# A four-layer recurrent and expert kernel: scan end by blocks, expert blocks early, gating of channel parts on GpSimd, shares applied after the hidden product

## The reference

```
# layer 0 mixer: sign-weight MLP, group quantisation, then a selective scan, 256 channels, 16 states
h = h * exp(dt * A) + (dt * x) * B          # per channel and state, along 1024 tokens
y = (sum over states of h * C + D * xs) * silu(z);   s = qx + y @ out_proj
# layer 0 ffn: 8 experts of three relu layers; v[e] = sum over tokens of y_e * w_e; g = ind @ v
# layer 1 mixer: two softmax-weighted sums over the tokens, then xn @ (Wq + diag(..) Wv.. Wr)
# layer 1 ffn: 8 experts, hidden 256, the best two of each token:
h = silu(xn @ Wgate_e) * (xn @ Wup_e);  g = sum over chosen e of share_e * (h @ W2_e)
```

## Time and profile before

| what | value |
|---|---|
| runs (median; all) | 1368.02 us; 1360.9, 1368.02, 1369.02 |
| the profiled execution | 1367.33 us, span 1365.3 us |
| TensorE busy | 1192.4 us (87%) |
| VectorE busy | 997.3 us (73%) |
| ScalarE busy | 801.6 us (59%) |
| GpSimd busy | 480.8 us (35%) |

### The profile page before, as it was taken

One profiled execution on the slowest core, in us unless ns is written; L12 is line 12 of the kernel. 1 busy time (PEld: TensorE's weight loads), 2 busy tenths in 40 slices (PEclk: granted clock), 3 DMA queues, 4 the chain that ended last, 5 costly groups with the idle time before them and its releaser, 6 DMA issues.

```text
span 1365.3 us, 14601 instructions
## 1 busy us (share of the span) xinstructions
PE 1192.4 (87%) x5025; PEld 626.3 (46%) x5025; DVE 997.3 (73%) x1432; ACT 801.6 (59%) x1097; POOL 480.8 (35%) x263
## 2 busy tenths in 40 slices
PE   5767599999985899999947999999999999798888
PEld 1322144444432444444525666666666666422454
DVE  4558799999986455533568899999899999623353
ACT  4344666676642434322466888888888888634542
POOL 9000188888876000000001354544544445500000
PEclk9879599999995899999778999999999999999999
DMA  3000255555531000000000000000000000000000
GB/s 115 0 3 6 89 182 183 180 192 188 183 137 47 0 0 1 1 0 0 0 0 16 14 14 21 15 21 14 14 21 14 21 14 14 1 0 0 1 0 31
DMA packets 26073, 59.90 MB, mean 44 GB/s; under 512 B 5544, under 2 KB 11080, under 8 KB 25736
## 3 DMA queue, kind: packets, MB, share of 16 engines
q1 hardware_dynamic: 26000, 58.97, 12.9%
HBM read 56.80 MB, written 1.38 MB: 43 GB/s over the span
## 4 chain that ended last, share of the span: by engine, by line
PE 41%; DVE 37%; ACT 15%; issue 5%; POOL 1%; DMA 0%; DVEq 0%; POOLq 0%; SPq 0%; ACTq 0%
DVE work L585 10%; DVE work L1371 6%; DVE work L1390 5%; ACT ps L487 5%; PE ps L869 5%; PE ps L877 4%; PE ps L1025 4%; PE ps L885 4%; ACT work L1232 3%; DVE yd L1435 3%; ACT work L1227 3%; PE ps L1066 2%; DVE work L1438 2%; PE ps L1626 1%; PE ps L235 1%
## 5 line engine op out<-in xcount | busy, mean ns | idle before, releaser
L1491 POOL TENSOR_TENSOR ssum<-ssum,rs 128x1024 f32<-128x1024 f32 x32 | 77.1, 2410 | 221.3 <-DVE work L1371 219.0
L585 DVE TENSOR_TENSOR_SCAN work<-ps,work 128x1024 f32<-128x1024 f32 x64 | 146.6, 2291 | 8.8
L605 POOL TENSOR_TENSOR work<-work 128x1024 f32<-128x1024 f32 x43 | 102.5, 2384 | 116.9 <-DVE work L585 116.9
L1371 DVE SCALAR_TENSOR_TENSOR work<-work,w_t 128x1024 f32<-128x1024 f32 x96 | 123.4, 1285 | 24.2 <-ACT work L1232 21.9
L409 PE MATMUL ps<-work,ident 128*128 128x512 f32 x256 | 123.0, 603 | 2.5 <-POOL work L605 2.4
L487 ACT ACTIVATE ps<-work,A 128x1024 f32<-128x1024 f32 x64 | 71.6, 1119 | 83.3 <-DVE work L585 81.7
L901 ACT ACTIVATE work<-ps 128x512 f32<-128x512 f32 x64 | 38.2, 597 | 110.8 <-PE ps L869 110.8
L1499 POOL TENSOR_TENSOR yd<-yd,work 128x896 f32<-128x896 f32 x32 | 67.3, 2102 | 72.9 <-DVE work L1438 72.9
L937 DVE TENSOR_TENSOR work<-work,ps 128x512 f32<-128x512 f32 x64 | 44.0, 688 | 57.0 <-PE ps L877 57.0
L1485 POOL MEMSET ssum<- 128x2048 f32 x1 | 1.8, 1804 | 237.2 <-DVE work L257 237.2
L1414 DVE SCALAR_TENSOR_TENSOR work<-work,ps 128x64 f32<-128x64 f32 x384 | 79.3, 276 | 6.2
(11 more groups left out here) (340 smaller groups left out, 2669.0 us busy)
## 6 DMA issues: line engine op xcount, KB each, us to landing
work<-bc_rows SPq DMA_DIRECT2D x43, 512.0 KB, 3.6
yd<-bc_rows SPq DMA_DIRECT2D x21, 512.0 KB, 3.5
rs<-w_rows SPq DMA_DIRECT2D x32, 256.0 KB, 3.4
w_t<-in_tile_w SPq DMA_DIRECT2D x32, 195.5 KB, 2.4
work<-in_w SPq DMA_DIRECT2D x1, 2048.0 KB, 9.6
shared<-in_f SPq DMA_DIRECT2D x3, 512.0 KB, 6.1
work<-in_x SPq DMA_DIRECT2D x4, 256.0 KB, 3.5
work<-in_w2e SPq DMA_DIRECT2D x1, 1024.0 KB, 11.6
```

Of the source, the lines that this page charges most:

```text
L585: dve.tensor_tensor_scan(h, flat_pair(DABANK), h, 0.0, ALU.mult, ALU.add).then_inc(m0["scan"], 1)
L605: pool.tensor_tensor(HS[u % 4], HS[u % 4], CB[u % 3], ALU.mult).then_inc(m0["state"], 1)
L1371: c = dve.scalar_tensor_tensor(HC[u], HP[:, tap:tap + SEQ], par(u, "taps", tap), HC[u], ALU.mult, ALU.add)
L1491: pool.tensor_tensor(ssum[:, b, :], ssum[:, b, :], rs[:, :, :].rearrange("p k t -> p (k t)"), ALU.add).then_inc(m2["ss"], 1)
```

## The change

1. Three expert blocks of layer 0 (`AHEAD` = 6 half steps) are computed before the loop, between the projection and the x_proj matmuls; ScalarE's relus of them stand around its silus of `XS`. In the loop all expert work runs six half steps ahead. The buffer r3 is doubled, and GpSimd weighs a block three units before ScalarE sums it.
2. Within the loop ScalarE scales `XS[:, j]` by D (at state 3), and GpSimd adds `DX` and multiplies by silu(z) for j = 0, 1, 2 while the next part is scanned (at its states 4 and 6). Part 3 is done by VectorE after the loop in two halves.
3. The end of the scan, out_proj, mix, gating and the second norm run block by block: blocks 0 and 1 first, blocks 2 and 3 inside the norm's steps (`first=`).
4. Layer 1: the bfloat16 share broadcast, `xw` and the split into parts are gone. The shares are turned with one transpose, stored to DRAM and loaded again, spread over the partitions, one 512-token row for each step; GpSimd multiplies the hidden product by them (128x1024) before the output matmuls, which now run five steps later (`LAG` = 5, eight hidden buffers). The gate and up matmuls of step 0 are issued inside the norm.
5. `stairs` is cut into 12 parts that GpSimd issues before its multiplication at even steps of the expert loop.
6. The expert weights of layer 1 are loaded as soon as the last decay is done; the last two gatings overlap the loop.

```diff
@@ l0_pe
+            for v in range(AHEAD):
+                f0_experts_pe(pe, v)
             for k in range(NB):
                 b, h = divmod(k, NB // BATCH)
                 pe.wait_ge(m0["act"], m0["xs"] + MI * (b + 1))
...
-                f0_experts_pe(pe, u)
+                f0_experts_pe(pe, u + AHEAD)
                 if u >= 1:
                     add_up(u - 1)
+            f0_turn_pe(pe)
+            for k in range(2):
+                f0_mix_pe(pe, k)
+            pe.wait_ge(m0["drive"], len(UNITS))
+            for k in range(2):
+                out_project(pe, k)
+            for k in range(2, NB):
+                f0_mix_pe(pe, k)
             add_up(len(UNITS) - 1)
@@ l0_act
+                if j == 0:
+                    for v in range(AHEAD // 2):
+                        f0_relus_act(act, v)
+                if j == 1:
+                    for v in range(AHEAD // 2, AHEAD + 1):
+                        f0_relus_act(act, v)
                 act.wait_ge(m0["dve"], m0["conv"] + j + 1)
                 act.activation(XS[:, j, :], DL[:, j, :], ACT.Silu).then_inc(m0["act"], 1)
...
+                if n == 3:
+                    j = MI * b + m
+                    act.activation(XS[:, j, :], XS[:, j, :], ACT.Copy, scale=V("d", m)).then_inc(m0["xs_scaled"], 1)
@@ l0_pool
+                if j >= 0 and n == 4:
+                    pool.wait_ge(m0["xs_scaled"], j + 1)
+                    pool.wait_ge(m0["act"], m0["sum_out"] + j + 1)
+                    pool.tensor_tensor(XS[:, j, :], XS[:, j, :], DX[:, j, :], ALU.add).then_inc(m0["y_sum"], 1)
+                if j >= 0 and n == 6:
+                    pool.wait_ge(m0["y_sum"], j + 1)
+                    pool.tensor_tensor(XS[:, j, :], XS[:, j, :], zgate[j % MI][:, (j // MI) * SEQ:(j // MI + 1) * SEQ],
+                                       ALU.mult).then_inc(m0["y_gated"], 1)
                 pool.wait_ge(m0["scan"], u + 1)
@@ new: l0_last_dve, l0_rest_dve (run inside the norm of layer 1)
+        def l0_last_dve(dve, own):
+            j = BATCH * MI - 1
+            dve.wait_ge(m0["ysum"], len(UNITS))
+            dve.wait_ge(m0["xs_scaled"], j + 1)
+            for h in range(NB // BATCH):
+                here = slice(h * BL, (h + 1) * BL)
+                own(dve.tensor_tensor(XS[:, j, here], XS[:, j, here], ps[:, YACC + h, :], ALU.add))
+                dve.tensor_tensor(XS[:, j, here], XS[:, j, here], zgate[MI - 1][:, ...],
+                                  ALU.mult).then_inc(m0["y_half"], 1)
+        def l0_rest_dve(dve, own, k):
+            if k == 1:
+                l0_last_dve(dve, own)
+            if k >= 2:
+                l0_out_dve(dve, own, k)
@@ new: l1_pool
+            for n in range(N1):
+                if n % 2 == 0 and n // 2 < STAIRS:
+                    stairs(pool, own, n // 2)
+                pool.wait_ge(f1["h"], 2 * (n + 1))
+                pool.wait_ge(share_in[n % len(share_bc)], 16 * (n // len(share_bc) + 1))
+                pool.tensor_tensor(hid[n % NH], hid[n % NH], share_bc[...].unsqueeze(1).to_broadcast([P, 2, BL]),
+                                   ALU.mult).then_inc(f1["weighed"], 1)
@@ l1_pe
+            norm_pe(pe, 3, X, f0["dve"], f0["x_out"], logits, rest)
+            pe.wait_ge(m1["dve"], m1["sub"] + 1)
+            l1_side_pe(pe, 0)
+            for n in range(1, N1 + LAG):
+                if n < N1:
+                    gates(n)
+                    ups(n)
+                if n == 1:
+                    pe.wait_ge(f1["dve"], f1["shared"] + 1)
+                    pe.transpose(ps[:, TURN_BANK, 0:P], by_expert, ident[:, :]).then_inc(f1["pe"], 1)
+                if n >= LAG:
+                    outputs(n - LAG)
                 l1_side_pe(pe, n)
@@ l1_dve
+            top2(dve, own, rw[:, 0], rt[:, :, 0:E])
+            hidden(0)
+            chosen_share(dve, own, rw[:, 0], 1e-6)
+            dve.tensor_tensor(by_expert..., rw[:, 1], bc(rm[:, 2, :]), ALU.mult).then_inc(f1["dve"], 1)
+            for n in range(1, N1):
+                hidden(n)
                 l1_side_dve(dve, own, n)
```

More of the change, by code:

```diff
@@ L212, in build @@
                     dve="sub:1 wk_scaled:2 wv_scaled:2 comb_out:2", each="soft_mm less_max exp weighted")
-        f1 = stages("f1", pe="picked_T:1", act="g:4", dve="picked:1 x_out:4", each="rt_out wbc xw gate silu up h y")
+        f1 = stages("f1", pe="shares_T:1", act="g:4", dve="shared:1 x_out:4", each="rt_out rows w_in0 w_in1 w_in2 w_in3 gate silu up h weighed y")
         m2 = stages("m2", pe="dt_mm:1 bc_mm:8 cum:1 tot:1 cumT:1 bt:4 gt:4 rms:4",
@@ L252, in norm_pe, with norm_dve @@
                     use(k)
-        def norm_dve(dve, own, r, src, dst, gain=None, bias=None):
+        def norm_dve(dve, own, r, src, dst, gain=None, bias=None, first=None):
             def scale(k):
@@ new lines, in l1_pe, with gates, ups, outputs @@
+        def l1_pe(pe):
+            def gates(n):
+                k, e = divmod(n, E)
+                for m in range(2):
+                    if n >= 1:
+                        pe.wait_ge(f1["silu"], 2 * (n - 1) + m + 1)
+                    c = e * 2 * I1 + m * P
+                    pe.matmul(ps[:, GATE_BANK[m], :], W["w13"][:, c:c + P], blk(XN, k), start=True, stop=True).then_inc(f1["gate"], 1)
+            def ups(n):
+                k, e = divmod(n, E)
+                for m in range(2):
+                    if n >= 1:
+                        pe.wait_ge(f1["h"], 2 * (n - 1) + m + 1)
+                    c = e * 2 * I1 + I1 + m * P
+                    pe.matmul(ps[:, UP_BANK[m], :], W["w13"][:, c:c + P], blk(XN, k), start=True, stop=True).then_inc(f1["up"], 1)
+            def outputs(q):
+                k, e = divmod(q, E)
+                if e == 0 and k >= 2:
+                    pe.wait_ge(f1["act"], f1["g"] + k - 1)
+                pe.wait_ge(f1["weighed"], q + 1)
+                for m in range(2):
+                    mm = pe.matmul(ps[:, Y_BANK[k % 2], :], W["w2e"][:, (2 * e + m) * P:(2 * e + m + 1) * P], hid[q % NH][:, m, :],
+                                   start=(e == 0 and m == 0), stop=(e == E - 1 and m == 1))
+                mm.then_inc(f1["y"], 1)
@@ L850, in logits @@
                     mm = pe.matmul(ps[:, SIDE, i * E:(i + 1) * E], tile(XN, i), W["router"], start=True, stop=True)
+                if k == 1:
+                    pe.wait_ge(load["experts"], 16 * len(EXPERTS))
+                    gates(0)
+                if k == 2:
+                    ups(0)
                 if k == NB - 1:
                     mm.then_inc(m1["pe"], 1)
[L854 to L856 removed]
```

378 lines of the change are left out of this document (194 added, 184 removed).

## The result

The changed kernel takes **1356.64 us** (median of 7 runs, 1352.57 to 1358.82) against 1367.74 us for the kernel before in the same session (7 runs, 1360.9 to 1370.24). The ratio is 0.9928, 95% interval 0.9905 to 0.9951: faster by 0.7%, clear of noise, but inside the 1% that the prediction counted as "the same" (it had given that 0.37, and 0.55 to faster by more). Forecast were 1353.0 us, a range of 1335 to 1370, and 15 us of gain; 11.1 us came. The profiled execution has a span of 1354.6 us (before: 1365.3).

The account below looks back on a forecast made before the run. It saw VectorE pacing the scan loop, no engine full from scan end to router, and matmuls bounding the expert loop; 2.2 + 3.2 - 14.5 - 5.5 - 0.3 = -15 us gave 1353 us, range 1335 to 1370.

Parts of the forecast that it names:

- A: Ahead of the scan: three expert blocks placed there delay x_proj and so VectorE; +2.2 us, between 0 and +6.
- B: Scan loop: pace stays, but lateness from GpSimd's added multiplications partly reaches VectorE; +3.2 us in sum.
- C: Scan end to router: block-by-block work takes 33.5 us in place of 48.0; -14.5 us, between -17 and -9.
- D: Router to the end of the expert loop: earlier start and shorter steps, less new waits; -5.5 us in all.
- E: Last gatings: three of four run before the last outputs; -0.3 us, between 0 and -2.
- the lock: Expert loop: VectorE's weighing of two SBUF operands waits for GpSimd's hidden multiplication; 8.2 us, between 0 and 19.
- The clock's +1.1: Expert loop: two falls of TensorE's clock cost +3.5 us, a warmer start gives -2.4; +1.1 us.
- (4): Expert loop: side work loses its one-step lead, so TensorE waits at eight steps for the weighing; 17.8 us.
- Rivals 1: Whole kernel: short steps overlap and nothing is held up; 19 us better, 1334; chance 0.30 together with halfway, 1344.
- 4 (1335): Expert loop: the eight waits don't exist since the weighing finishes earlier; 17.8 us better, 1335; chance 0.05.
- Rival 3: Expert loop: the clock falls after each of eight waits, 41 us in place of 3.5; 1391, slower; chance 0.08.
- Rival 2: Expert loop gives back nearly everything: GpSimd's lock costs 19 us, scan-to-router gains only 11; 1367, no change; chance 0.20.

Follow-up runs that it names:

- e8: Changed kernel with the removed constant selr (a memset and three selections on GpSimd) put back at the start, used by nobody: 1358.64 us.
- e6: Changed kernel with the addition and gating of parts 0 to 2 moved from GpSimd's loop to VectorE behind the last scan: 1356.38 us.
- e16: Changed kernel with 3 and 4 extra matmuls, results unused, in TensorE's two waits of the second norm: 1345.97 us.
- e2: Changed kernel with expert 0's gate and up matmuls of layer 1 issued behind the whole second norm: 1353.08 us.
- e3: Changed kernel without GpSimd's multiplication of the hidden product by the shares: 1338.02 us (1 run).
- e11: Changed kernel with e1, e2 and e10's edits, constant sel2 built in the expert loop, and the softmax weighing ahead of VectorE's hidden product: 1324.77 us.
- e1: Changed kernel with expert n+1's gate matmuls issued in iteration n of layer 1's expert loop, ahead of ups(n): 1352.81 us.
- e17: Changed kernel with e10's products and the softmax weighing ahead of VectorE's hidden product, gate matmuls still in their own step: 1349.46 us.
- e10: Changed kernel with the two softmax products of each block replaced by four 128x128 operations that read PSUM: 1348.59 us.
- e14: Changed kernel with 6 and 8 extra matmuls, results unused, in TensorE's two waits of the second norm: 1357.34 us.

## Why the prediction was right and where it was wrong

The time lies in the range and in my own case (1346 to 1360), but the sum came this close partly by luck. Against their forecasts A came 3.3 us better and B 2.5, and C came 8.4 worse; D and E together were 0.4 off, and the two stages that I had put at nothing came 2.7 worse and 1.5 better.

**A** was right, from another starting point. x_proj was forecast near 121, 7.6 later than the earlier trace rows; it came at 116.60, but its convolution had started 4.4 us earlier (98.30 for 102.75), so against that it is 7.7 later. VectorE's delay at the first scan is 3.4 us against the earlier start, for a forecast of 2.2. **What I left out** is the 4.4: I noted the removed selections only between scan end and router and not at the program's start, where the earlier trace rows had shown what GpSimd's work does to a product of two SBUF tiles. e8 gives 3.4 us of it back; the other 1.0 stays open.

**B** was too high, +3.2 for +0.7. The add-up waits for GpSimd ten times (8.0 us; five times and 4.5 us in e6, without the gating), but VectorE's drives wait 1.0 us in all. I had the cover too small: 1.2 us from the state to its add-up and 1.6 or 1.05 from the spread to its drive add up to 2.8 or 2.2, not to 1.7 to 2.2, and the lateness that I expected was 2.6. e6 puts the loop's price of the gating at 1.2 us. In the text on what bounds the kernel, TensorE was busy longer than VectorE in this loop (225.21 and 218.04 us), not nearly as long.

**C** is the step that failed: -14.5 forecast, -6.1 measured, outside its own bounds of -17 and -9 and past my sign of being wrong ("if C stays above 40 us"; it took 41.9). Two parts:
- The clock. I allowed 2 us for matmuls at 1.2 GHz, "fewer than before, since TensorE has more to do here". The changed kernel lost 1.7 at the first out-projection and about 4.2 from 414.89 to 423.5, after two waits that I did not have. Where these were filled (e16) the stage took 36.0, with the first out-projection fast as well.
- A wait in VectorE's queue. Blocks 2 and 3 are added behind the scaling of blocks 0 and 1 (L259), and each scaling waits 1.93 us for ScalarE's square, logarithm and exponential. It is a matter of order again: the variance of block 0 was ready at 402.0, but ScalarE takes the square of block 1 first (403.47), and that waits for VectorE's subtraction (402.76). I wrote "subtraction and scaling (1.4)" and counted no wait. My steps end at 418.3, 31.8 us behind 386.5 (so the sum with allowance should have been 33.8, not 33.5); two of these waits, 3.9 us, would make that 35.7, close to e16's 36.0. These waits were read off the trace; no run removed them:

```profile
405.37 0.69 DVE L259 TENSOR_TENSOR work<-work,rs 128x512 f32<-128x512 f32 x1 [1.93 <-ACT rs L282]
405.97 0.68 DVE L625 TENSOR_TENSOR work<-ps,work 128x512 f32<-128x512 f32 x1
...
412.02 0.69 DVE L259 TENSOR_TENSOR work<-work,rs 128x512 f32<-128x512 f32 x1 [1.93 <-ACT rs L282]
412.63 0.68 DVE L625 TENSOR_TENSOR work<-ps,work 128x512 f32<-128x512 f32 x1
```

That gates(0) ahead of the last variance costs something (1.7 in my sum) was right: the clock made 3.71 of it, and e2's edit won 1.8 us in the stage, and lost as much in the loop. That the constants' absence would help here the two traces bear out: VectorE's eight gating products took 1.46 to 1.57 us each before (L755, L756), beside GpSimd's selections, and 0.69 in the changed kernel (L811, L812); that is 6.6 us of VectorE's work, though no run tells how much of it lay on the path. I also read that no engine is full from 386.5 on; VectorE was busy for 12.76 of the first 12.90 us.

**D** was right in sum, and in the mechanism of its waits. The ups of step 1 start 6.6 us after the router's reduction (434.60 less 428.03; forecast 6.6). A clean step takes 5.15 us (forecast 5.15). The waits are 22.6 us (forecast 26): 16.1 for the queues' order (17.8) and 6.5 for the lock (8.2, though my own terms add up to 7.9). In e3, without the lock, the eight waits are 3.29 us twice and 1.6 six times, where I had 3.5 twice and 1.8 six times. The table load went as the sum had it: it starts at 455.06 and takes 1.28 us, and the exponential starts at 456.35 (both rows stand in the time line shown with the result). The drain of 1.38 us behind it, of the Trainium skill, page ScalarE: Activation LUTs, section What ACT_TABLE_LOAD costs, does not show here either. The clock's +1.1 was too small: the gates took 68.4 us in all against 62.3 in e11, where nothing waits, so about 6 us on these matmuls alone; this error and that of the waits nearly cancel. But my account of (4) was incomplete: "the side work loses its lead" names one cause where there are two. e1 gave the lead back and the waits stayed (21.7 us); e17 changed VectorE's order and they stayed (16.8, as in e10); both together left 3.0.

**E** was right in size (-0.5; the last outputs end 0.7 us before the last gating, 1.2 before the change). What I did not forecast is 2.7 us in layer 2's norm, which the diff does not touch.

Rivals 1 (1334) and 4 (1335) fell with the waits. Rival 3 (1391) fell too: the granted clock was 0.85 from 440 to 475, behind the two longest waits (5.09 and 3.69 us), 1.00 from 475 to 540 in spite of waits of 2.1 to 2.8 us, and 0.95 from 540 to 575. Rival 2 foretold C's shortfall and the wrong reason for the total, since the lock came in at 6.5 and not at 19 us.

**Open:** layer 2's norm took 17.2 to 23.2 us with the same instructions in all runs, and "the rest" 687.2 to 688.1 or 690.6 to 691.0. The norm's lengths go with the granted clock over it: 0.69 for 23.2 us (changed, where a row of eight L1235 takes 1.75 us instead of 1.08), 0.78 for 20.5 (e14), 0.86 for 19.1 (e1), 0.90 for 18.9 (e11), 0.95 for 17.6 (e2) and 0.98 for 17.2 (e16). Which earlier event decides it was not isolated. It is worth up to 6 us, so medians of edits elsewhere carry it (e1, e2, e3, e6, e11, e16), and their stages say more than their totals.

## What to carry to other kernels

When one engine waits for a chain, list every queue that the chain passes and what stands ahead of it there: two queues can each hide the other, and then undoing either alone shows nothing. Count removed work of GpSimd wherever VectorE multiplies two SBUF tiles beside it, or give VectorE an operand in PSUM, and the collision is gone. A wait of TensorE can also cost the speed of what follows; short matmuls that just fit the wait can buy that back, and their length has to be measured first. And before a stage's gain is put down to an edit, compare the matmuls ahead of the edit: where they differ too (3.70 and 5.39 us here), that part is the clock's.

## What the runs showed of the hardware

- Seven matmuls whose results nobody uses, 6.4 us of TensorE work in two waits of 2.8 and 3.9 us, kept the clock at 1.00 there and made the stretch behind them 4.2 us shorter (e16); fourteen, 12.4 us, kept the clock up too, but the stage came out at 42.6 us for 41.9 (e14).
- A 128x512 float32 matmul with float32 weights shows as two instructions and took 0.89 us at 2.4 GHz.
- A 128x128 scalar_tensor_tensor with one source in PSUM took 0.348 us each of 32 times beside GpSimd's 128x1024 product. Four of them (1.50 us with their gaps) replace 1.41 us of undisturbed or up to 3.2 us of disturbed two-step work.
- The same code was granted 0.57 of the clock between 412 and 424 us in one execution and 0.86 in another (the changed kernel and e3), and layer 2's norm, with the same instructions, 0.69 to 0.98.
